# Attention with three-pass products on one core: the two transpose groups of a cell are issued one after the other, and the filling products of a step are cut in two parts

## The reference

```
q = rope(x @ Wq.T)                      32 heads of 128
c_kv = x @ Wdk.T ; k = mix(rope(x @ Wkr.T), c_kv @ Wupk.T) ; v = c_kv @ Wupv.T     8 key/value heads
attn = softmax(causal(q @ k.T / sqrt(128))) @ v ; y = attn @ Wo.T
x1 = layernorm(x + y)
out = layernorm(x1 + (silu(x1 @ W1.T) * (x1 @ W3.T)) @ W2.T)      W1, W2, W3 unpacked from 4-bit values
```

## Time and profile before

| | |
|---|---|
| median of 3 runs | 2422.88 us (2419.59 to 2423.49) |
| the profiled execution, its own time | 2424.2 us |
| its span, first to last instruction | 2422.4 us |
| PE busy | 2381.3 us, 98% |
| ACT busy | 1626.7 us, 67% |
| DVE busy | 1440.9 us, 59% |
| POOL busy | 573.8 us, 24% |
| mean granted TensorE clock | 0.995 of full speed |

### The profile page before, as it was taken

One profiled execution on the slowest core, in us unless ns is written; L12 is line 12 of the kernel. 1 busy time (PEld: TensorE's weight loads), 2 busy tenths in 40 slices (PEclk: granted clock), 3 DMA queues, 4 the chain that ended last, 5 costly groups with the idle time before them and its releaser, 6 DMA issues.

```text
span 2422.4 us, 40379 instructions
## 1 busy us (share of the span) xinstructions
PE 2381.3 (98%) x12028; PEld 1999.1 (83%) x12028; DVE 1440.9 (59%) x3752; ACT 1626.7 (67%) x3213; POOL 573.8 (24%) x441
## 2 busy tenths in 40 slices
PE   8999999999999999999999999999999998899998
PEld 6888888888888888888888888888888876778886
DVE  5334666666666666666666666666666676842332
ACT  4223878787887878787878878787878774322211
POOL 3002313132231313131322313132313203400000
PEclk9999999999999999999999999999999999999999
DMA  7767433333242423332332424242323335421110
GB/s 262 277 216 290 136 105 114 101 108 128 88 160 82 147 82 134 100 116 98 110 126 90 160 78 152 79 138 96 121 95 112 122 102 158 136 86 35 52 35 18
DMA packets 110934, 293.43 MB, mean 121 GB/s; under 512 B 10784, under 2 KB 27680, under 8 KB 101600
## 3 DMA queue, kind: packets, MB, share of 16 engines
q1 hardware_dynamic: 110880, 292.73, 36.4%
HBM read 208.80 MB, written 88.08 MB: 123 GB/s over the span
## 4 chain that ended last, share of the span: by engine, by line
PE 90%; DVE 4%; DMA 2%; issue 2%; ACT 1%; SPq 1%; POOL 0%; DVEq 0%; POOLq 0%; ACTq 0%
PE b_ps L260 43%; PE b_sps L260 31%; PE b_tps L1502 10%; PE b_tps L1552 2%; PE b_ps L1552 2%; PE b_tps L260 1%; DVE c_sl L1242 1%; DMA c_sl<-in_s2p 1%; DVE c_pk L1263 1%; DMA b_xs<-xs_d 0%; DVE c_pk L1253 0%; DMA a_raw<-in_wkrT 0%; ACT b_sc L958 0%; ACT b_pt L979 0%; DMA b_kt<-k_d 0%
## 5 line engine op out<-in xcount | busy, mean ns | idle before, releaser
L1217 DVE TENSOR_TENSOR b_pt<-b_tps,b_pt 128x512 fp32r<-128x512 f32 (+3 forms) x768 | 427.0, 556 | 295.6 <-ACT b_pt L979 289.3
L979 ACT ACTIVATE b_pt<-b_tps 128x512 fp32r<-128x512 f32 (+3 forms) x768 | 369.4, 481 | 193.3 <-PE b_tps L1502 190.7
L260 PE MATMUL b_sps<-b_kt,b_qs 128*128 128x512 f32 (+4 forms) x2304 | 497.4, 343 | 0.4 <-DMA b_kt<-k_d 0.4
L260 PEld LDWEIGHTS b_sps<-b_kt,b_qs 128*128 128x128 f32 x2304 | 402.9, 188 | 55.9 <-issue 1.7
L964 ACT ACTIVATE b_sc<-b_sc,b_rinv 128x896 f32<-128x896 f32 (+7 forms) x512 | 396.8, 775 | 65.6 <-DVE b_rinv L1207 58.2
L260 PE MATMUL b_ps<-b_xs,b_wq 128*128 128x512 f32 x1536 | 440.8, 406 | 0.1
L260 PE MATMUL b_ps<-b_pt,b_vt 128*128 128x512 f32 x1584 | 436.1, 403 | 2.1 <-DVE b_ys L1228 1.5
L260 PE MATMUL b_ps<-b_wo,b_ot 128*128 128x512 f32 x1536 | 422.4, 405 | 1.2 <-DVE b_ys L1228 1.2
L958 ACT ACTIVATE b_sc<-b_sc,b_nmax 128x896 f32<-128x896 f32 (+7 forms) x512 | 395.4, 772 | 29.1 <-DVE b_nmax L1199 28.8
L1199 DVE CUSTOM_DVE_ANT_0 b_sc<-b_sps,b_mask 128x896 f32<-128x896 f32 (+7 forms) x512 | 386.8, 755 | 19.7 <-PE b_sps L260 19.7
L1502 PE MATMUL b_tps<-b_ident,b_sc 128*128 128x128 f32 x2304 | 374.0, 272 | 4.2 <-DVE b_pt L1217 4.2
(11 more groups left out here) (137 smaller groups left out, 2283.4 us busy)
## 6 DMA issues: line engine op xcount, KB each, us to landing
b_xs<-xs_d SPq DMA_DIRECT2D x32, 2048.0 KB, 9.0
b_ys<-y_d SPq DMA_DIRECT2D x128, 256.0 KB, 2.6
y_d<-b_ys SPq DMA_DIRECT2D x128, 256.0 KB, 2.8
k_d<-a_ks SPq DMA_DIRECT2D x32, 512.0 KB, 4.0
v_d<-a_vs SPq DMA_DIRECT2D x32, 512.0 KB, 3.0
b_kt<-k_d SPq DMA_DIRECT2D x64, 256.0 KB, 4.4
b_vt<-v_d SPq DMA_DIRECT2D x16, 1024.0 KB, 4.8
b_wraw<-in_wqT SPq DMA_DIRECT2D x64, 256.0 KB, 2.7
```

The source lines that it names most:

```text
L260: ins = nc.tensor.matmul(out, *every[n], start=(n == 0), stop=(n == len(every) - 1))
L979: nc.scalar.activation(pt[:, u % PT_UNITS, HI, 0:nj, h * P:(h + 1) * P], tps[n % 2][:, 0:nj], ACT.Copy)\
L1217: nc.vector.tensor_tensor(pt[:, u, LO, 0:nj, h * P:(h + 1) * P], tps[n % 2][:, 0:nj], pt[:, u, HI, 0:nj, h * P:(h + 1) * P], ALU.subtract) ...
```

## The change

The third and fourth rows of PE's order lose the products between the two pieces, and `SHARES[2]` has two equal parts. Since `SHARES[2]` is shared, steps 1 and 2 change too, although their row of the order stays.

```diff
-            ("scores", "fill", 0, "fill", 1, "fill"),
-            ("scores", "fill", 0, "fill", 1, "fill"))
-
-SHARES = ((1,), (0, 1), (1, 1.25, 1))
+            ("scores", "fill", 0, 1, "fill"),
+            ("scores", "fill", 0, 1, "fill"))
+
+SHARES = ((1,), (0, 1), (1, 1))
```

## The result

| | before | changed |
|---|---|---|
| median of the runs | 2423.05 us (6 runs, 2419.59 to 2424.75) | 2433.93 us (6 runs, 2431.49 to 2436.82) |
| ratio | | 1.0042, 95% interval 1.0031 to 1.0054 |
| the profiled execution, its own time | 2424.2 us | 2431.5 us |
| its span | 2422.4 us | 2429.7 us |
| idle time of the transposes that ended with DVE | 4.2 us | 10.0 us |

The change makes the kernel 0.4% slower, 10.9 us by the medians. The profiled execution of the changed kernel is the fastest of its six runs, so its own time shows less of the difference than the medians do. Where the loss sits has to be read inside the turns.

What follows compares the result with a forecast made beforehand. PE's issued work was taken to bound the kernel. The terms 0 + 10.4 + 1.8 made 12.2 us, so 2422.9 became 2435.1 us, 0.5% slower, with a range of 2427 to 2442.

Steps and rivals of the forecast that it cites:

- What bounds the kernel: PE's issued work sets the time; reordering gains only if that work shortens and loses wherever a wait appears.
- part 1: All 240 merged pairs: eight transposes in a row cost what two fours do; price 0, plus or minus 5 us.
- Part 2: Steps 1 and 2: products moved ahead of the first pieces cost PE 0.69 us at 15 boundaries, 10.4 us.
- The hand-over from p46 to p0: From step 2's first piece to the piece behind step 3's scores: a fixed 2.01 us through ACT and DVE.
- The start of p47: Step 2's second piece waits for DVE's end of step 1's second piece, starting 0.06 us behind it, 0.31 later.
- Part 3: Steps 19 to 31: only step 20 is tight; its second piece waits, losing 1.8 us over 11 turns.
- The room that was read for steps 21 to 31: Second piece's slack to DVE's part two pieces earlier: at least 0.87 us at step 21, over 1.7 from 22.
- The sign that was named for part 1 being wrong: Eight merged transposes taking under 0.84 us would show the zero price of merging to be wrong.
- That the switch counts: Rival, faster: each merged pair saves 0.087 us of late product start, 20.9 us over 240 pairs; chance 0.04.
- That the waits stay covered: Rival, no change: ACT, DVE or slack at step 0 absorb the delays, 2422 to 2427 us; chance 0.11.
- More waits in steps 19 to 31: Rival, slower still: first pieces' delays pass to queries and weights, 16 x 0.46 us more, 2442; chance 0.05.
- The mean clock: Rival: clock falls to 1.2 GHz over the merged groups, doubling each pair's 0.89 us, 2637 us; chance 0.01.

Runs made afterwards that it cites:

- experiment 4: Only step 1 changed (8/0/0 products, step 2 left at 6/2/0's neighbour 6/3/0), in the kernel before: 2428.20 us, ratio 1.0021.
- experiment 6: Step 2 moved the other way, to 5/4/0 products from 6/3/0, in the kernel before: 2422.21 us, ratio 1.0001.
- experiment 7: Steps 1 and 2 moved the other way, to 5/3/0 and 5/4/0 products, in the kernel before: 2422.96 us, ratio 0.9998.
- experiment 1: The changed kernel with steps 1 and 2 put back as before, so only steps 19 to 31 changed: 2423.62 us, ratio 1.0001 to the kernel before.
- experiment 10: The changed kernel with three of step 3's six products put ahead of its scores: 2426.08 us, ratio 1.0013 to the kernel before.
- experiment 9: Kernel before, first piece of steps 22 to 31 cut in halves with one product between, 160 more transpose groups: 2422.96 us, ratio 1.0007.
- experiment 2: Only steps 1 and 2 changed (8/0/0 and 9/0/0 products), in the kernel before: 2431.30 us, ratio 1.0032.
- experiment 3: Only step 2 changed (9/0/0 products), in the kernel before: 2432.26 us, ratio 1.0035.
- experiment 5: Step 2 at 8/1/0 products, a smaller dose than the change, in the kernel before: 2429.05 us, ratio 1.0025.

## Why the prediction was right

**What bounds the kernel: right.** PE's busy time is 2381.3 us before and 2382.3 after; the order changed PE's own work by little (part 1, below), and each new wait was paid in full.

**Part 2, steps 1 and 2: right in place and in size.** 0.69 us a boundary was forecast and 0.669 measured by the mean, 0.695 by the median turn; the 15 boundaries make 10.0 us for 10.4. The hand-over from p46 to p0, read as 2.01 us, is 2.01 to 2.02 at 14 of the boundaries after the change too, and 2.10 at the last. The start of p47 0.06 behind DVE's p45 is as forecast, and p47 behind p46 by 0.76 for 0.75. Two readings on the way were off, and neither touched the forecast. ACT was taken to be free for p46 at 1237.14 at the latest. It makes good 0.16 of its delay (experiments 4 and 6). p46 was later than that anyway, but the expectation for step 1 alone came out too high by it (0.46 for 0.32). And p0 was said to be 0.16 us late in the kernel before, against the 0.36 us of step 4's scores. Those follow a product; scores that follow transposes take 0.44, so p0 was 0.08 late, and PE would be ready for it at 1238.29 in place of 1238.21, still far ahead of 1238.75. With the slower start of the products behind a p0 that waited (0.08 us behind it, for 0.03 where nothing waits), the hidden wait is worth about the 0.14 to 0.15 that experiments 6 and 7 win in step 3.

**Part 3, step 20: right in its mechanism, and in size for this execution.** 1.8 us was forecast and 16 x 0.103 = 1.6 measured. p19 starts 0.05 to 0.06 us behind DVE's end of p17 in 8 turns, where 11 were forecast to lose time. The same step 20 loses 0.071 a turn in the profile of experiment 1 and 0.047 in that of experiment 10, 1.1 and 0.8 us in all. How much is lost differs from one execution to the next, so that the 1.6 came so near is in part luck. The timeline of the changed kernel at a turn whose weights land late shows the wait inside the merged group, as five transposes that take until 1735.81 (0.64 us where five in a row would be 4 x 0.11 + 0.03 = 0.47). The timelines of PE and of DVE: DVE ends p17 at 1735.38 + 0.29 = 1735.67, and p19, the last of the five, can start only behind that:

```profile
1735.17 0.88 PE L1502 MATMUL b_tps<-b_ident,b_sc 128*128 128x128 f32 x5
1735.81 1.17 PE L260 MATMUL b_ps<-b_pt,b_vt 128*128 128x512 f32 x4
```
```profile
1735.38 0.29 DVE L1217 TENSOR_TENSOR b_pt<-b_tps,b_pt 128x128 fp32r<-128x128 f32 x1 [1.24 <-ACT b_pt L979]
```

The room that was read for steps 21 to 31 held.

**Part 1, the merge itself: the term that was mis-sized.** "Price 0", with bounds of 0.02 us a pair, was -0.20 us a turn in steps 21 to 30, 3.2 us in all, or 0.02 for each of the 160 pairs there. It lies at the edge of the bounds. The argument for 0 (a merged group costs what two do) holds. In step 31 of the changed kernel the product behind eight transposes starts 0.79 us after the first of them and takes 0.314; behind four in the kernel before it is 0.354 and 0.316. With 0.227 taken off for a product in a stream, eight cost 0.88, and two fours 0.89. The sign that was named for part 1 being wrong, under 0.84, is not there. The gain has another source, below. This gain, the 0.6 us of step 31 and the small excess of parts 2 and 3 pull the sum by the steps to 7.9 us; the forecast was 12.2. The medians say 10.9, nearer to the forecast than the steps are. Nothing in the prediction accounts for that nearness, so it counts as luck; the interval holds both.

**The rivals.** That the switch counts is refuted by experiment 9. That the waits stay covered is refuted by experiments 2 to 5. More waits in steps 19 to 31 are not there beyond step 20. The mean clock is 0.995 in both profiles, and 1.00 over the eight merged transposes of step 31 in the four turns that were read (1225.95 to 1226.74 is one), so it did not fall with the longer groups. The Trainium skill (TensorE: Matmul & The Clock Gate, PE-mode transpose) says that transposes don't count as PE-busy for the clock in the same way. By that a drop was possible, and the measurement decides.

## What to carry to other kernels

When a buffer is handed round a loop of engines, find the loop's time (here PE to ACT to DVE and back to PE, 2.0 us) and count what the issuing engine has to do inside it. Moving work from inside the loop to ahead of it costs that work's whole time once the loop is exposed, even on an engine that is busy for 98% of the span and even if no instruction is added; putting other work in front of the waiting instruction gives most of it back. Work moved the other way wins only as much as the instruction had waited, and here the next tight place took two thirds of that. Where a constant is shared between steps, read the timeline at each step that uses it: here the loss sat in two steps whose order was not the one being edited.

## What the runs showed of the hardware that was not expected

The products of the same shape do not all take the same time. In step 28 of a turn, the kernel of experiment 1 runs six of them from 1206.31 to 1207.67, 0.227 us each, ahead of the transposes, and the six behind them take 1.47:

```profile
1206.31 1.53 PE L262 MATMUL b_ps<-b_wo,b_ot 128*128 128x512 f32 x6
1207.67 0.93 PE L1504 MATMUL b_tps<-b_ident,b_sc 128*128 128x128 f32 x7
1208.35 1.63 PE L262 MATMUL b_ps<-b_wo,b_ot 128*128 128x512 f32 x6
1209.82 0.40 PE L262 MATMUL b_ps<-b_pt,b_vt 128*128 128x512 f32 x1
```

1.47 less the 0.087 by which the first behind transposes is longer is 0.230 each. Over turns 3 to 15, the products of step 26 ahead of the first piece go at 0.230 to 0.236 in the kernel before and at 0.226 to 0.227, all but the last, in that of experiment 1. Step 26 is the one with the largest gain, 0.043 us. Summed over steps 21 to 30 of these turns, the changed kernel spends 0.83 us a turn more from the starts of transposes to what follows them and 0.99 less on products, and 0.04 less on scores. The merge as such explains a shift of 0.83 from one to the other: ten times a first product behind transposes is saved, 0.315 for 0.232. What is left, 0.16 in products and 0.04 in scores, is the gain. It is thus in how fast products and scores follow each other, not in the transposes. What decides it (more scores and products in a row without a group between, or where in its three passes a run is cut) is open; the runs don't tell these apart.
